# Root parts in PSUM from block 3 on, one transpose for the first slot, seven late rows, first high parts on ScalarE, another order in the tail

## What is computed

```python
q = _l2norm(proj(Wq)); k = _l2norm(proj(Wk)); v = proj(Wv)
attn = jnp.einsum('bhqd,bhkd->bhqk', q, k)
rel = pos[None, :] - pos[:, None]
mask = (rel < 0) | (rel >= WINDOW)                  # WINDOW = 128
bias = jnp.where(mask[None], NEG_INF, -jnp.abs(rel)[None] * slopes[:, None, None])
attn = jax.nn.softmax(attn + bias[None], axis=-1)
out = jnp.einsum('bhqk,bhkd->bhqd', attn, v)        # then @ Wo.T
x = _layernorm(x + attention(x))
h = jax.nn.gelu(jnp.einsum('bsd,hd->bsh', x, bw1) + b1, approximate=False)
x = _layernorm(x + jnp.einsum('bsh,dh->bsd', h, bw2) + b2)
```

## Time and profile before

| what | value |
|---|---|
| median of 3 runs | 374.02 us (373.98 to 376.59) |
| the profiled execution's own time | 376.11 us |
| its span in the trace | 374.4 us |
| busy: PE, DVE, ACT, POOL | 339.0, 310.9, 293.5, 268.9 us |
| share of the span | 91%, 83%, 78%, 72% |
| PE in the granted clock's mean | 0.974 |

### The profile page before, as it was taken

How to read it: one execution, slowest core, us unless ns; L and a number is a source line. 1 busy time by engine, 2 the same in 40 slices (tenths; PEclk the granted TensorE clock), 3 DMA queues, 4 the chain that set the end, 5 groups by cost and what they waited for, 6 DMA issues and landing times.

```text
span 374.4 us, 12297 instructions
## 1 busy us (share of the span) xinstructions
PE 339.0 (91%) x4269; PEld 229.8 (61%) x4269; DVE 310.9 (83%) x777; ACT 293.5 (78%) x494; POOL 268.9 (72%) x314
## 2 busy tenths in 40 slices
PE   8798599899899899899898798696999999999992
PEld 6554366667666566567575566453566666667682
DVE  5978879889989989989989959989777887887875
ACT  2597478889889889888989979584788888888753
POOL 1167679988989979979889967574557757856433
PEclk9999699999999999999999989898999999999998
DMA  7576656746646656677777655002203514404113
GB/s 229 130 136 153 141 89 115 154 99 137 144 92 143 129 108 142 156 153 171 170 155 165 108 100 103 12 16 43 51 7 60 88 32 109 109 21 95 56 57 115
DMA packets 106882, 40.16 MB, mean 107 GB/s; under 512 B 92128, under 2 KB 105824, under 8 KB 106720
## 3 DMA queue, kind: packets, MB, share of 16 engines
q1 hardware_dynamic: 106848, 39.73, 48.8%
HBM read 12.72 MB, written 4.19 MB: 45 GB/s over the span
## 4 chain that ended last, share of the span: by engine, by line
PE 30%; DVE 10%; ACT 4%; issue 3%; DMA 2%; POOL 2%; SPq 1%; DVEq 0%; POOLq 0%; ACTq 0%
PE ps L555 13%; PE ps L588 13%; DMA qkT<-parts 2%; ACT prob L694 2%; PE ps L435 1%; PE ps L454 1%; SPq L285 1%; DVE stats L901 1%; DVE resid L972 1%; DVE w L1168 1%; DVE faded L927 1%; ACT parts L674 1%; POOL prob L1347 1%; POOL parts L1367 1%; PE ps L402 1%
## 5 line engine op out<-in xcount | busy, mean ns | idle before, releaser
L1347 POOL TENSOR_SCALAR_AFFINE_SELECT prob<-prob 128x1024 f32<-128x1024 f32 x126 | 136.6, 1110 | 25.2 <-ACT prob L694 25.0
L694 ACT ACTIVATE prob<-ps 128x1024 f32<-128x1024 f32 (+1 forms) x128 | 121.9, 1007 | 12.8 <-PE ps L402 12.8
L425 PE MATMUL ps<-prob,faded 128*17 128x128 f32 x2016 | 62.6, 277 | 2.7 <-issue 1.4
L764 ACT ACTIVATE ps<-ps,bias,alpha 128x512 f32<-128x512 f32 x64 | 47.9, 750 | 21.8 <-PE ps L555 18.7
L435 PE MATMUL ps<-wqkv,xt 128*128 128x512 f32 x124 | 62.9, 630 | 1.1 <-DVE qkn L963 1.1
L555 PE MATMUL ps<-yT,sgn 128*128 128x512 f16 x256 | 62.4, 384 | 0.3 <-DVE w L1168 0.2
L425 PEld LDWEIGHTS ps<-prob,faded 128*17 128x17 f32 x2016 | 53.2, 99 | 9.6 <-issue 5.8
L402 PE MATMUL ps<-qkT 64*64 64x192 f16 (+2 forms) x1024 | 35.8, 249 | 13.9 <-DMA qkT<-parts 7.7
L1415 POOL TENSOR_TENSOR resid<-z,resid 128x256 f32 (+1 forms) x31 | 22.5, 726 | 30.4 <-DVE z L1178 30.4
L402 PEld LDWEIGHTS ps<-qkT 64*64 64x64 f16 x1024 | 20.5, 106 | 35.3 <-issue 34.6
L555 PEld LDWEIGHTS ps<-yT,sgn 128*128 128x128 f16 x256 | 24.8, 99 | 25.8 <-DVE w L1168 2.2
(11 more groups left out here) (114 smaller groups left out, 595.6 us busy)
## 6 DMA issues: line engine op xcount, KB each, us to landing
xt<-in_xT SPq DMA_DIRECT2D x32, 128.0 KB, 2.3
resid<-in_x SPq DMA_DIRECT2D x32, 128.0 KB, 2.4
out_dram<-resid SPq DMA_DIRECT2D x7, 512.0 KB, 3.0
w<-in_w2T SPq DMA_DIRECT2D x1, 1024.0 KB, 8.1
w<-in_w1T SPq DMA_DIRECT2D x4, 256.0 KB, 3.4
w_nat<-in_w SPq DMA_DIRECT2D x4, 256.0 KB, 4.1
wqkv<-in_wqkvT SPq DMA_DIRECT2D x3, 256.0 KB, 4.4
qkT<-parts SPq DMA_TRANSPOSE x39, 4.3
```

Source lines behind the costliest of these rows:

```text
L425: mm = nc.tensor.matmul(ps[32 * m:32 * m + HD + 1, OT, P * c:P * c + P], v, p, start=(n == 0), stop=(n == 1 or not near))
L694: nc.scalar.activation(to, scored, ACT.Exp, scale=QK_SCALE ** -2).then_inc(exp_done, 1)
L764: nc.scalar.activation(bank, bank, ACT.Gelu, bias=bias1[:, k:k + 1], scale=alpha1[:, k:k + 1]).then_inc(gelu_done, 1)
L1347: return nc.gpsimd.affine_select(out=at, in_=at, compare_op=ALU.is_ge, fill=0.0, base=-near, pattern=[[0, 2 * CH], [1 if near else -1, P]] ...
```

## The change

It does five things. (1) `in_psum` holds from step 0 on, so the seeds and rounds of blocks 3 and later use PSUM; `seeds_of(3)` stands behind `fade_values(1, 1)`, and `project_v` waits for the round from block 2 on. In the written-out first steps `double` of blocks 3 to 5 goes from VectorE to ScalarE, `fade_values(3, 3)` stands in front of `turn_sums(0)`, and `scale_sums(0)` behind `normalise_rows(5, 1)`. (2) `rden` lies in the PSUM bank `VO` for blocks 0 to 27, and every `project_v(n)` waits for `onorm_done` of n - 3 (line 873 of VectorE's step). (3) The second transpose and its semaphore go; for slot 0 the scores read slots 3 and 0 with a negative step, 256 columns wide instead of 192. (4) LATE is 7: rows 25 and 26 leave `round_of` / `y_row` of steps 30 and 31, and norm_of leaves ScalarE's steps 29 to 31. (5) In the tail ScalarE makes all eight first high parts, and TensorE's and VectorE's code there stand in another order.

```diff
-LATE = 5
+LATE = 7
-FIRST_BY_ACT = (1, 3, 5, 6, 7)
+FIRST_BY_ACT = tuple(range(HC))
-        qkT = sb("qkT", [P, 2 * (H // 2), XS + 1, P], F16)
+        qkT = sb("qkT", [P, 2 * (H // 2), XS, P], F16)
+        rden_in_psum = ps[:, VO, D + 192:D + 192 + H]
         def in_psum(i, next3):
-            return next3 and (not isinstance(i, int) or i >= 4)
+            return next3 and (not isinstance(i, int) or i >= 0)
...
-                if s == 0 and not (isinstance(n, int) and n == 0):
-                    sp.dma_start_transpose(qkT[:, 0:H // 2, XS, :],
-                                           parts[:, 0, 0:H].rearrange("p h a d -> p (h a d)")).then_inc(again_in, 16)
...
-                    if slot == 0:
-                        count(pe, again_in, again)
...
+                            if both and slot == 0:
+                                first, last, moving = 0, 2 * P, queries[:, XS - 1::1 - XS, :]
+                            else:
+                                at = (slot - 1) * P if both else -P
+                                moving = queries.rearrange("p s q -> p (s q)")[:, at + first:at + last]
...
                 count(pe, v_ready, n)
-                if not isinstance(n, int) or 6 <= n < NB - 1:
+                if not isinstance(n, int) or 2 <= n < NB - 1:
                     pe.wait_ge(newton, norm_base(n - 2, True) + NORM_OPS)
+                count(pe, onorm_done, n - 3)
...
             for c in range(NC):
                 weighted_sum(NB - 2, c, 2)
+            hidden(0, 4, 0)
             project_late(NB - 3)
-            hidden(0, 4, 0)
-            hidden(0, 5, 0)
             for c in range(NC):
                 weighted_sum(NB - 1, c, 3, near=False)
+            hidden(0, 5, 0)
             project_late(NB - 2)
...
-            step(1, 1, ln=False, squares_first=True, doubled=False)
+            step(1, 1, ln=False, squares_first=True)
...
-            step(NB - 3, 1, next3=False, before_rows=lambda: signs2(1), tail=lambda: high_y(1, 1, 1))
-            step(NB - 2, 2, next2=False, next3=False, before_rows=last_signs)
+            step(NB - 3, 1, next3=False, ln=False, before_rows=lambda: signs2(1), tail=lambda: high_y(1, 1, 1))
+            step(NB - 2, 2, next2=False, next3=False, ln=False, before_rows=last_signs)
...
+                to = rden[:] if isinstance(q, int) and q >= NB - 4 else rden_in_psum
...
-                if not prev3 and prev_ln:
-                    round_of(i - 1, False, True)
...
-                if ln:
-                    row_stats(i - 4, mv)
+                late_row_of = i - 4 - (NB - LATE) if isinstance(i, int) else -1
+                row_stats(i - 4, mv if late_row_of < 0 else mv_late[:, late_row_of, :])
...
+            late_stats(NB - 4)
+            turn_sums(NB - 2)
             hidden_low(0, 0, 0)
-            round_of(NB - 2, False, True)
-            y_row(NB - 6, False)
-            row_stats(NB - 5, mv_late[:, 0, :])
-            outputs(NB - 2)
+            scale_sums(NB - 2, 0)
             add_output(NB - 3, late=True)
             hidden_low(0, 1, 0)
-            row_stats(NB - 4, mv_late[:, 1, :])
-            row_stats(NB - 3, mv_late[:, 2, :])
             hidden_low(0, 2, 0)
-            outputs(NB - 1)
+            turn_sums(NB - 1)
+            hidden_low(0, 3, 0)
+            scale_sums(NB - 1, 1)
             add_output(NB - 2, late=True)
```

More of the change, by code:

```diff
@@ L696, in step @@
                 if high_first:
[L697 removed]
+                    high_halves(i + 2, par)
                 exps(0)
@@ L812, in _ @@
             act.wait_ge(abs_done, 9)
+            high_hidden(0, 0, 0)
             high_hidden(0, 1, 0)
             gelu_of(0, 2, 0)
+            high_hidden(0, 2, 0)
             high_pair()
[L816 to L824 removed]
+            for k in range(3, HC):
+                gelu_of(0, k, 0)
+                high_hidden(0, k, 0)
             activate(1, 1)
@@ L867, in scale_sums @@
             def scale_sums(q, par):
+                to = rden[:] if isinstance(q, int) and q >= NB - 4 else rden_in_psum
                 dve.wait_ge(sums_turned, q + 1)
-                nc.vector.reciprocal(rden[:], turned[:, :, HD]).then_inc(rden_done, 1)
+                nc.vector.reciprocal(to, turned[:, :, HD]).then_inc(rden_done, 1)
                 dve.wait_ge(rden_done, q + 1)
@@ L1066, in _ @@
             sums_of(3)
-            seeds_of(3, False)
             double(2, 0)
             fade_values(1, 1)
+            seeds_of(3, False)
             round_of(0, True, False)
             normalise_rows(3, 1)
+            sums_of(4)
             fade_values(2, 2)
-            sums_of(4)
             seeds_of(4, False)
-            double(3, 1)
             round_of(1, True, False)
@@ L1080, in _ @@
             sums_of(5)
+            fade_values(3, 3)
             seeds_of(5, False)
-            double(4, 0)
+            turn_sums(0)
             round_of(2, True, False)
-            outputs(0)
             normalise_rows(5, 1)
-            fade_values(3, 3)
+            scale_sums(0, 0)
             sums_of(6)
+            fade_values(4, 0)
             seeds_of(6, False)
-            fade_values(4, 0)
-            double(5, 1)
             step(4, 0, prev_ln=False)
@@ L1216, in finish_first @@
                         hidden_low(1, k, 1)
-                    if b > 1:
-                        late_row(b - 2)
+                    if b > 0:
+                        late_row(b - 1)
                     if b > 0:
```

76 lines of the change are left out of this document (23 added, 53 removed).

## The result

| | before | changed |
|---|---|---|
| median | 374.75 us (373.98 to 376.59, 4 runs) | 360.69 us (355.97 to 362.6, 4 runs) |
| profiled execution, span | 376.11, 374.4 us | 361.29, 359.6 us |
| busy: PE, DVE, ACT, POOL | 339.0, 310.9, 293.5, 268.9 us | 336.1, 294.5, 296.5, 267.6 us |

The ratio is 0.958, 95% interval 0.947 to 0.968: faster by 4.2% (3.8% between the medians), where the forecast of 351.4 us was 6% and its range ended at 357. Ratios leave out executions more than 1.5% above the fastest of their kernel: here the one of 362.6 us, and in the experiments, among others, one of 434.97 us of the kernel before (granted clock 0.748) and one of 560.49 us of a2_stt (0.56). The changed kernel's executions are spread unevenly: three lie at 360 to 363 us, one at 355.97.

A forecast was written before the change was run, and what follows sets the result against it. TensorE bounds the last 109 us, so gains come earlier, where start, loop, steps 25 to 28 and tail have different bounds. 7.0 + 4.1 + 3.5 + 2.7 + 3.8 + 1.5 = 22.6 us off 374.0 gives 351.4 us, range 347 to 357.

The forecast's parts named there:

- `rden` in PSUM: Loop steps: `otok` falls from 0.58 to 0.42 us, the row of y ends when it did; gain 0, at most 3 us.
- Steps 24 to 29: End of attention: TensorE's 2.25 us transpose wait goes and step 28 falls from 8.12 to 6.88 us; gain 3.5 us.
- The new wait of `project_v`: TensorE in each step: a ring through this wait of 6.1 to 6.3 us, shorter than 6.57; cost 0.
- Loop: Steps 5 to 24: without the transpose wait, steps of 6.57 us set by the ring from VectorE's seeds to the next; gain 4.1 us.
- 256 columns: Slot 0's scores on TensorE: at worst 2.4 us more over seven steps, but covered by spare time; cost 0.
- The 1.2 us of step 7: TensorE's wait of 1.22 us in step 7, which nothing in the change removes, kept in the loop's 126.0 us.
- Start: First steps: ScalarE sets the pace at 6.0 us a step, step 4's exponentials begin at 41.5 us; gain 7.0, 3 to 7.6.
- Late rows and tail order: Step 30 and the tail: seven late rows gain 2.7 us, the reordered tail 3.8 and fewer VectorE high parts 1.5.
- The rival in which ScalarE takes the lead: Tail: ScalarE becomes the bound and only 4 of 8 us are gained there, 355.4 us; chance 0.10.
- loop stays: Loop: steps remain at 6.85 us, total gain 18.5 and time 355.5 us; chance 0.12.
- start gives 3: First steps: the gain is 3 us instead of 7, time 355.4 us; chance 0.12.

The follow-up runs named there:

- a2_stt: e2_hidden with the row of y written as a scalar_tensor_tensor with a broadcast second operand instead of a tensor_scalar; 360.92 us.
- a1_rden_sbuf: The changed kernel with `rden` in SBUF for every block and nothing else changed; 356.22 us, ratio 0.948 to the kernel before.
- b1_small: e2_hidden with a small 128x32 multiplication between SBUF tensors on VectorE in front of every row of y; 377.03 us, one run.
- e2_hidden: The changed kernel with TensorE's first hidden chunk moved behind the weighted sums of step 29; 359.11 us, ratio 0.956 to the kernel before.
- e1_gap: The changed kernel with GpSimd waiting ahead of its step 5 for the first row of y; 357.15 us, ratio 0.950 to the kernel before.
- b4_best: The changed kernel with `rden` in SBUF, no new `project_v` wait, e2_hidden's move, and GpSimd's low halves of block 7 ahead of step 5's first selects; 352.33 us.
- e3_both: The changed kernel with the edits of both e1_gap and e2_hidden; 354.42 us, ratio 0.943 to the kernel before.
- c3_again: b4_best with the second transpose for slot 0, its semaphore and the 192-column scores brought back; 362.52 us.
- c4_roots_sbuf: b4_best with the root parts of blocks 3 to 6 put back in SBUF; 356.48 us.
- b2_tail_only: The kernel before with only parts (4) and (5) of the change; 367.28 us, ratio 0.981 to the kernel before.

## Why the prediction was right and wrong

**`rden` in PSUM: the step that failed, with the row of y.** The prediction took 0 for it, because the row "ends when it did", at the end of the select that runs. In the loop the 0 was right: `otok` is at 0.42 us as forecast, and `rden` back in SBUF changed 12 steps by 0.1 us. The row was at 0.62 and 0.66 us in steps 15 and 16 (I had said 0.8) and does end 0.15 us behind its select, but what swallows `otok`'s gain is another wait, for TensorE's `project_out`. VectorE waits for it 19 times, 7.6 us in all, against 7 times and 5.2 us in a1_rden_sbuf. In step 15:

```profile
122.67 2.18 POOL L1320 TENSOR_SCALAR_AFFINE_SELECT prob<-prob 128x1024 f32<-128x1024 f32 x2 [0.53 <-ACT prob L685]
122.95 0.42 DVE L882 TENSOR_TENSOR resid<-resid,ps 128x256 f32 x1 [0.21 <-PE ps L450]
123.29 0.62 DVE L955 TENSOR_SCALAR resid<-resid,mv,rnorm  x1
```

In step 5 it was wrong. GpSimd had run without a gap for 24 us there, and the row waited not for one select but until GpSimd ran dry, up to 5.9 us. So the term was a loss of 4.5 to 5.1 us (a1_rden_sbuf), outside my bounds of 0 and 3 us gain. The Trainium skill (SBUF — State Buffer, Who interferes with whom), on which I leaned, says that the later one of the two blocks for one whole instruction of the other. The measurement decides: here it was six instructions, 5.87 us. Its other sentence, that issue order and not the shape of the operation decides, agrees with a2_stt and b1_small as to the shape. As to the order it doesn't: the row had asked before five of the six instructions began, and they went ahead of it. I had read the row from steps of the loop, where GpSimd has a gap of about 0.5 us in every step, and carried it to step 5, where it has none.

**Steps 24 to 29: the size right, the consequence missed.** The gain of 3.5 us measured 3.7, and step 28 lasted 7.03 us (6.9 forecast). I never asked what the 2.25 us of waiting had covered. Before, `yT`'s transposes were issued 1.6 us into step 28 and TensorE needed them 7.0 us later, without a wait:

```profile
215.68 2.27 SPq L341 DMA_TRANSPOSE yT<-yparts  x1
...
222.70 1.04 PE L555 MATMUL ps<-yT,sgn 128*128 128x512 f16 x4
```

Now they are issued 3.7 us into it, and the hidden chunk stands 6.6 us behind them with 2.45 us of it idle. The 2.25 us are the difference: counted from where TensorE was free for step 28, the issue came 3.8 us later before and 3.7 now. Cost of this: 2.2 us alone (e2_hidden), 2.7 on top of e1_gap. It is a transfer that becomes late next, and the prediction named none here.

**The new wait of `project_v`: nearly 0, as forecast.** TensorE waits for `otok` five times, 1.7 us in all, 0.75 of it behind the shut-out row. b4_best, without the wait, has 6.54 us a step against 6.60 with it (a1_rden_sbuf), 1.0 us over 17 steps. The waits in the loop add up to 0.95 us, which fits. b4_best also differs in GpSimd's order, so this is an estimate of the wait's price.

**Loop: right.** 6.60 us a step (6.57 forecast), VectorE's seeds 6.58 us apart from step 9 to 24, no wait on transposes in steps 8 to 24. 256 columns took 0.63 us per sixteen instead of 0.53; hidden, as taken. The 1.2 us of step 7 that I left in stayed: e3_both waits 1.75 us there, the changed kernel hides it behind the longer loss.

**Start: the pace right, the size too small.** Step 4 came 9.0 us sooner, where 7.0 was forecast and 7.6 was the most. ScalarE is full, as taken: from 22.05 to 42.9 us it has no gap, and its exponentials come 5.87 us a step apart (6.0 taken). They began at 22.05 us, not at 22.9, and those of step 4 at 39.67, not at 41.5. The prediction didn't look at GpSimd, which at this pace is full as well (17.87 of the 17.90 us from 25.4 on). c3_again shows 2.8 of the 9.0 us to be the second transpose of block 4, which I had priced only from the loop on; c4_roots_sbuf gives the roots 1.3 there and 4.2 by step 7. The other 4.9 us belong to the values, the doubles and the earlier order, which weren't tried one by one.

**Late rows and tail order: right.** 8.0 us forecast; 7.6 us in b2_tail_only's trace, 8.3 between the medians. The rival in which ScalarE takes the lead would have left 4.

**In sum** the terms other than `rden`'s were near (e3_both's span 351.3 against 351.8), and the miss is two waits that the prediction didn't have. That the sum is so near is partly luck: in e3_both the start gave 1.5 us more by step 5 than forecast (8.5), and steps 5 to 24 1.1 less (3.0), for the wait at step 7 and a slightly longer loop. The rivals "loop stays" and "start gives 3" put the time at about 355.5 us, nearer to the 360.7 measured, but neither happened.

## What to carry to other kernels

Where VectorE and GpSimd both use SBUF, look for the stretch in which GpSimd is behind and has no gap: an SBUF operation of VectorE on the path may wait there for the gap, not for the next instruction. Freeing an earlier operation from SBUF can open this trap, since it moves the moment at which the next one asks. Here one short wait of GpSimd gave 4.2 us back, of the 4.5 to 5.1 that a shorter operation of VectorE had cost. And when a wait of one engine is removed, list what the others finished in it: the next transfer (`yT` here) had its whole lead from that wait.
